# A GRU and block attention kernel: input tiles loaded first, the bias broadcast by DMA and added in PSUM

## The reference

```
gi = x_t @ W_ih + b_ih;   gh = h @ W_hh + b_hh           # 512 -> 1536 each
r = sigmoid(i_r + h_r);   z = sigmoid(i_z + h_z)
n = tanh(i_n + r * h_n);  h = (1 - z) * n + z * h        # 64 steps, one after another
x = x + hs
block = sum of x over 8 steps;  keys = rms_norm(block @ Wk.T) * rms_weight
attended = softmax(keys . cond[1]) over the blocks, applied to block
x = x + layernorm(x + attended @ Wo.T) * gamma + beta
```

## Time and profile before

| | us |
|---|---|
| median of three runs | 376.84 |
| the profiled execution | 376.77 |
| its span on the core, first to last instruction | 374.7 |
| TensorE busy in the span | 362.5 |
| VectorE, ScalarE, GpSimd busy | 262.6, 161.8, 16.1 |

### The profile page before, as it was taken

The page is one execution under the profiler, slowest core; times in us unless marked ns, Lnnn a source line. Parts: engine busy times, 40 slices in busy tenths (PEclk is TensorE's granted clock), DMA queues, the critical chain, the costliest instruction groups (busy, mean ns, idle before and its releaser), DMA issues.

```text
span 374.7 us, 9838 instructions
## 1 busy us (share of the span) xinstructions
PE 362.5 (97%) x3285; PEld 213.6 (57%) x3285; DVE 262.6 (70%) x1137; ACT 161.8 (43%) x512; POOL 16.1 (4%) x50
## 2 busy tenths in 40 slices
PE   7999999999999999999999999999999999997894
PEld 4465556666555566665556666555566665434662
DVE  3725667767676877686768767676878676778896
ACT  3702226262434344362526262434344364866510
POOL 7002000000000000000000000000000000100000
PEclk9999999999999999999999999999999999999999
DMA  5975535323232322324142323232232323110047
GB/s 186 396 298 119 159 96 163 101 70 100 73 97 71 74 73 67 101 52 113 34 108 49 98 70 98 70 98 70 58 89 67 101 52 78 42 42 20 21 169 280
DMA packets 27484, 38.63 MB, mean 103 GB/s; under 512 B 2988, under 2 KB 19016, under 8 KB 27464
## 3 DMA queue, kind: packets, MB, share of 16 engines
q1 hardware_dynamic: 27432, 38.36, 35.3%
q10 hardware_dynamic: 32, 0.01, 0.0%
HBM read 18.17 MB, written 4.19 MB: 60 GB/s over the span
## 4 chain that ended last, share of the span: by engine, by line
PE 92%; DVE 5%; issue 1%; DMA 1%; ACT 0%; DVEq 0%; SPq 0%
PE gates_ps L619 43%; PE gi_ps L587 37%; DVE gcx L1117 1%; PE first_ps L680 1%; PE first_ps L619 1%; PE fourth_ps L619 1%; PE third_ps L619 1%; PE keys_ps L619 1%; PE third_ps L680 1%; PE keys_ps L680 1%; PE fourth_ps L680 1%; DMA h_tok<-hist 1%; DVE w_hh L1032 1%; PE gi_ps L601 1%; PE keys_ps L747 1%
## 5 line engine op out<-in xcount | busy, mean ns | idle before, releaser
L619 PE MATMUL gates_ps<-w_hh,turned 128*32 128x384 f32 x1920 | 167.3, 489 | 0.5 <-DVE turned L840 0.5
L619 PEld LDWEIGHTS gates_ps<-w_hh,turned 128*32 128x32 f32 x1920 | 56.5, 109 | 85.5 <-issue 56.4
L587 PE MATMUL gi_ps<-w_ih_hi,xt_hi 128*128 128x384 f32 x240 | 87.3, 364 | 0.0
L587 PE MATMUL gi_ps<-w_ih_hi,xt_lo 128*128 128x384 f32 x240 | 81.2, 338 | 0.0
L587 PE MATMUL gi_ps<-w_ih_lo,xt_hi 128*128 128x384 f32 x240 | 80.2, 334 | 0.0
L480 ACT ACTIVATE rz<-gates_ps 128x256 f32<-128x256 f32 x60 | 23.0, 384 | 128.8 <-PE gates_ps L619 128.7
L904 DVE TENSOR_TENSOR rz<-gates_ps,rz 128x128 f32<-128x128 f32 x60 | 17.5, 292 | 79.5 <-ACT rz L480 79.5
L587 PEld LDWEIGHTS gi_ps<-w_ih_hi,xt_hi 128*128 128x128 f32 x240 | 45.0, 187 | 37.5 <-issue 37.5
L587 PEld LDWEIGHTS gi_ps<-w_ih_lo,xt_hi 128*128 128x128 f32 x240 | 45.1, 188 | 0.0
L587 PEld LDWEIGHTS gi_ps<-w_ih_hi,xt_lo 128*128 128x128 f32 x240 | 45.0, 187 | 0.0
L840 DVE STREAM_TRANSPOSE turned<-hist 128x32 f32<-128x32 f32 (+1 forms) x192 | 36.8, 217 | 2.2
(11 more groups left out here) (224 smaller groups left out, 301.1 us busy)
## 6 DMA issues: line engine op xcount, KB each, us to landing
gi<-gi_tok SPq DMA_DIRECT2D x60, 192.0 KB, 3.4
x1t<-in_x_t_dram SPq DMA_DIRECT2D x16, 256.0 KB, 3.2
gcx<-in_x_tok_dram SPq DMA_DIRECT2D x16, 256.0 KB, 3.2
h_tok<-hist SPq DMA_DIRECT2D x64, 64.0 KB, 2.2
out_dram<-gcx SPq DMA_DIRECT2D x16, 256.0 KB, 2.1
gcx<-in_w_ih_dram SPq DMA_DIRECT2D x4, 768.0 KB, 7.4
w_hh<-in_w_hh_dram SPq DMA_DIRECT2D x4, 768.0 KB, 9.1
wo_t<-in_wo_t_dram SPq DMA_DIRECT2D x1, 1024.0 KB, 5.6
```

Of the source, the lines that this page charges most:

```text
L587: mm = pe.matmul(gi_ps[tok][:, 0:G3], a[:, k, :], w[:, k, gi_cols(j)], start=(k == 0 and a is xt_hi and w is w_ih_hi), stop=(k == NJ - 1 a ...
L619: mm = pe.matmul(gates_bank(t)[j * B:(j + 1) * B, P:], before[:, k * B:(k + 1) * B], chunk(w_hh, k, j), start=False, stop=(k == NJ - 1), s ...
```

## The change

1. SP no longer waits first. Its order is: x's first quad, `W_ih` quarters 0 and 1, four broadcast transfers of the bias (32 partitions of 768 floats, 96 KB each), `W_ih` quarter 2, x's second quad, `W_ih` quarter 3, `cond`. `W_hh` and `b_in` follow as before; behind `b_hh_rz` stand six more transfers of constants (four of 64 KB, one of 512 KB, one of 256 KB).
2. The selection matrices, the small loads, the constants on TensorE and the copies of them are gone, the `lay_pick` between steps 0 and 1 too. TensorE has seven matmuls on zeros (L650) in place of three.
3. The first projection accumulates onto zeros. When quarter 1 has been added to bank t, VectorE adds the bias to it in place; TensorE waits for that before it adds quarter 2.
4. VectorE's order: low part of quarter 0, the sum of two bias parts, the four additions, low part of quarter 1, x's low part, low parts of 2 and 3, the turns of the first state. ScalarE rounds x before quarter 3. `gi_chunk(4)` takes the products with W's low part last, each behind a wait for its quarter.
5. `wq` and `wq_rec` are multiplied on GpSimd after its `b_in` sums; the waits on them, and the turn of beta, come later (step 3 in the first block). `br_all` and `br_t` lose a block that nothing wrote.

The core of the diff:

```diff
 # SP
-            sp.wait_ge(bias_made, 1)
-            sp.dma_start(bias_rows[0:NJ, 0:G3], b_ih_d).then_inc(bias_in, 16)
...
             sp.dma_start(x1t[:, 0], x_t_d[:, 0:NJ, :]).then_inc(x_first_in, 16)
             load_w_ih(0)
+            load_w_ih(1)
+            for j in range(NJ):
+                sp.dma_start(bias_in_rec[j * B:(j + 1) * B, :], bias_d[j:j + 1, :].broadcast_to([B, 6 * P])
+                             ).then_inc(bias_in, 16)
+            load_w_ih(2)
+            load_x_t(1)
+            load_w_ih(3)
             sp.dma_start(hist[:, S - 1, :], cond_d).then_inc(h0_in, 16)
-            load_w_ih(1)
-            load_w_ih(2)
-            load_w_ih(3)
-            load_x_t(1)
...
+            for j in range(NJ):
+                sp.dma_start(recs[j * B:(j + 1) * B].rearrange("p c u -> p (c u)"),
+                             recs_d[j:j + 1, :].broadcast_to([B, 4 * P])).then_inc(consts_in, 16)
+            sp.dma_start(tok_consts[:].rearrange("p c n -> p (c n)"), rows_d[None, 0:2 * D].broadcast_to([P, 2 * D])
+                         ).then_inc(consts_in, 16)
+            sp.dma_start(rms_tok, rows_d[None, 2 * D:].broadcast_to([P, D])).then_inc(consts_in, 16)
             move_gi(0, -1)
 # GpSimd
-            pool.memset(own_rows, 0.0).then_inc(pick_made, 1)
...
+            pool.tensor_tensor(wq, wq, rms_tok, ALU.mult).then_inc(wq_ready, 1)
+            pool.tensor_tensor(wq_rec, wq_rec, rms_rec, ALU.mult).then_inc(wq_ready, 1)
 # TensorE
-                if first and s == 0:
-                    lay_pick(small_ps, 2)
...
-            keep_warm(2)
...
-            keep_warm(1).then_inc(pe_warmed, 1)
+            keep_warm(7).then_inc(pe_warmed, 1)
...
+                    if k == 2:
+                        pe.wait_ge(first_seeded, t + 1)
                     for j in range(NJ):
...
+                    if k == 1:
+                        mm.then_inc(first_laid, 1)
...
-            gi_chunk(Q, Q, 1)
+            pe.wait_ge(w_hi_ready, NJ)
+            gi_chunk(Q, Q, 1, lo_last=True)
 # VectorE
+            split_w(0)
+            dve.wait_ge(bias_in, 16 * NJ)
+            dve.tensor_tensor(bias_rec[:, P:3 * P], bias_rec[:, P:3 * P], bias_in_rec[:, D:], ALU.add
+                              ).then_inc(bias_summed, 1)
+            dve.wait_ge(bias_summed, 1)
+            for t in range(Q):
+
+                dve.wait_ge(first_laid, t + 1)
+                dve.tensor_tensor(first_ps[t][:], first_ps[t][:], bias_rec, ALU.add).then_inc(first_seeded, 1)
+            split_w(1)
+            split_x(1)
+            split_w(2)
+            split_w(3)
             dve.wait_ge(h0_in, 16)
             for c in parts:
                 dve.transpose(turned[:, S - 1, c], hist[:, S - 1, c]).then_inc(ht_ready, 1)
-            for k in range(NJ):
-                split_w(k)
-            split_x(1)
```

More of the change, by code:

```diff
@@ L66, in gru_block_attention @@
         scalar_warm = sb("scalar_warm", [P, 1])
[L68 to L71, removed]
+        tok_consts = sb("tok_consts", [P, 2, D])
+        gamma_tok, wq = tok_consts[:, 0, :], tok_consts[:, 1, :]
+        recs = sb("recs", [P, 4, P])
+        gamma_rec, beta_rec, wq_rec, rms_rec = (recs[:, c, :] for c in range(4))
         beta_t = sb("beta_t", [P, P])
@@ L239, in steps @@
             def steps(i, first=False, last=False):
+                if last:
+                    sp.wait_ge(wq_ready, 2)
                 for s in range(S):
@@ L584, in gi_chunk @@
                 wait(pe, gi_tok_ready, idx - 1 - Q)
-                for k in range(NJ):
[L586 to L589, removed]
+                terms = ((xt_hi, w_ih_hi), (xt_hi, w_ih_lo), (xt_lo, w_ih_hi))
+                order = [(k, a, w) for k in range(NJ) for a, w in terms]
+                if lo_last:
+                    order = [(k, a, w) for a, w in (terms[0], terms[2], terms[1]) for k in range(NJ)]
+                for m, (k, a, w) in enumerate(order):
+                    if lo_last and w is w_ih_lo:
+                        pe.wait_ge(w_lo_ready, k + 1)
+                    mm = pe.matmul(gi_ps[tok][:, 0:G3], a[:, k, :], w[:, k, gi_cols(j)], start=(m == 0),
+                                   stop=(m == 3 * NJ - 1))
                 mm.then_inc(gi_done, 1)
@@ L651, in keep_warm @@
                 return mm
-            def lay_pick(bank, c):
-                for j in range(NJ):
-                    mm = pe.matmul(bank[:, j * P:(j + 1) * P], pick[:, j, :], const_rows[:, c, :],
-                                   start=True, stop=True)
-                mm.then_inc(consts_laid, 1)
-            keep_warm(2)
-            pe.wait_ge(pick_made, 4)
-            pe.wait_ge(bias_in, 48)
-            pe.matmul(first_ps[0][:], own_rows, bias_rows, start=True, stop=True).then_inc(bias_laid, 1)
-            pe.wait_ge(pick_made, 5)
-            pe.wait_ge(wq_row_ready, 1)
-            pe.matmul(gi_ps[0][:, 0:3 * P], own_rows, const_rows[:, 0:3, :], start=True, stop=True
-                      ).then_inc(consts_laid, 1)
-            lay_pick(gi_ps[1], 0)
-            keep_warm(1).then_inc(pe_warmed, 1)
+            keep_warm(7).then_inc(pe_warmed, 1)
             pe.wait_ge(x_first_in, 16)
@@ L1166 @@
     b_hh = by_chunk(inputs["L0_cond_b_hh"], (0, 1, 2))[0]
+    b_ih = by_chunk(inputs["L0_cond_b_ih"], (2, 0, 1)).reshape(NJ, G3)
+    rms, gamma, beta = (inputs[f"L1_cond_{name}"] for name in ("rms_weight", "ln_gamma", "ln_beta"))
     laid_out = {
@@ L1172 @@
         "w_ih": by_chunk(inputs["L0_cond_W_ih"], (2, 0, 1)).reshape(D, 3 * D), "w_hh": inputs["L0_cond_W_hh"],
-        "b_ih": by_chunk(inputs["L0_cond_b_ih"], (2, 0, 1)).reshape(NJ, G3),
-        "b_hh": _np.concatenate([b_hh[:, 0:2].reshape(-1), b_hh[:, 2].reshape(-1)]),
-        "rms_weight": inputs["L1_cond_rms_weight"],
+        "b_ih": b_ih,
+        "b_hh_rz": b_hh[:, 0:2].reshape(-1),
+        "bias": _np.concatenate([b_ih, b_hh[:, 2], b_hh[:, 0], b_hh[:, 1]], axis=1),
+        "recs": _np.concatenate([a.reshape(NJ, P) for a in (gamma, beta, cond[1], rms)], axis=1),
+        "rows": _np.concatenate([gamma, cond[1], rms]),
         "wk_t": inputs["L1_cond_Wk"].transpose(1, 0), "wo_t": inputs["L1_cond_Wo"].transpose(1, 0),
-        "gamma": inputs["L1_cond_ln_gamma"], "beta": inputs["L1_cond_ln_beta"],
     }
```

102 lines of the change are left out of this document (28 added, 74 removed).

## The result

| | before | after |
|---|---|---|
| median of the runs on one chip, 22 each | 377.37 us (376.36 to 378.64) | 375.72 us (375.10 to 377.35) |
| profiled execution | 376.77 us | 375.67 us |
| its span | 374.7 us | 373.5 us |
| TensorE's share of the chain | 92% | 85% |
| step 0 ends on TensorE | 25.07 us | 23.56 us |

The ratio on record is 0.9965, interval [0.9956, 0.9975]: 0.35% faster. The interval leaves out a ratio of 1, but the gain lies under the 0.5% that the prediction set as its bound for a change that one measurement of this kernel can tell. (The two medians stand 1.65 us apart, 0.44%.) I had put the likeliest time at 374.7 and "faster by over 0.5%" at 0.60; the median of the changed kernel lies one microsecond above that.

What follows compares the result with a forecast made beforehand. The prediction had TensorE and the DMA stream finish step 0 together, the `W_hh` transfers setting its end after the change. 1.25 (step 0) + 0.89 (`lay_pick`) = 2.14 us off 376.77 gave 374.63, stated as 374.7; range 372.8 to 376.1.

Steps and rivals of the forecast that it cites:

- the bound of step 0: Opening: the last quarter of `W_hh` lands at 22.95 us, so step 0 ends at 23.8 against 25.07, 1.25 earlier.
- TensorE's own path: Opening: TensorE's work alone, if nothing makes it wait, would end step 0 at 22.3 us.
- The `lay_pick`: Between steps 0 and 1: 0.89 us of TensorE with nothing beside it goes in full.
- The term of the bias: DMA stream ahead of `W_hh`: four bias transfers cost 1.3 us, with 0.98 and 2.8 as the ends.
- SP's start: Opening: SP issues x first, at 0.71 instead of 3.26 us, so x and quarter 0 land 2.55 earlier.
- the TensorE rival: Opening: a shorter DMA tail leaves TensorE as the bound, step 0 ending at 22.3 to 22.5, 373.2 us; chance 0.25.
- GpSimd's two products: Behind the opening: the two products fall in idle time of GpSimd and cost nothing.
- The prediction's list of signs: Wrong if, among others, `rz` L904 of step 1 is held by GpSimd or TensorE waits longer on VectorE than on `W_hh`.
- The slack of `b_in`: Before VectorE's `rz` of step 1: slack falls from 1.4 to 0.5 us, so `b_in` stays covered.
- The constants: Queue behind `b_in`: six transfers, 2.6 us, ahead of the first `move_gi`, which has until step 4.
- the bias was dear: Rival, DMA stream: bias transfers at 140 GB/s cost 2.8 us, leaving a gain of 0.64, 376.2 us; chance 0.21.
- `b_in` was not late: Rival, step 1: constants delay `b_in` by 3.8 us, making the kernel 1.2 us slower, 378.0; chance 0.04.

Runs made afterwards that it cites:

- the first experiment: The changed kernel with GpSimd's two products held until VectorE has made six projected rows: 375.47 us, ratio 0.9954; run again, 374.36 us.
- one-transfer kernel: The changed kernel with the same 0.39 MB of bias as one transfer to 128 partitions, rows repeated in DRAM: 375.83 us, ratio 0.9967.
- the first combined version: Changed kernel with one bias transfer, `b_in` and its summand in two halves, fourth sum behind the third kept rows, products later: 374.11 us, ratio 0.9916.
- the last version: The first combined version with constants issued in step 4, beta turned in step 6 and GpSimd's products in step 8: 374.13 us, ratio 0.9913.

## Why the prediction was half right

**What held.** SP's first issue came at 0.74 (forecast 0.7). `W_hh` was the bound of step 0, which ended at 23.56 (forecast 23.8), and TensorE's own path stood where it was put: 22.47 in the run without the bias, for 22.3. The `lay_pick` went in full: 0.89. Step 1 began at 25.84 (forecast 26.1), 2.42 us earlier where the sum said 2.14. Behind step 1 all steps but one kept the lengths that they had.

**The term of the bias was too small, and another gain made up for it.** I took 1.3 us between 0.98 and 2.8; the runs give 1.86. With SP's start alone, 2.55 earlier, that would have left 0.7 at the `b_in` issue; measured were 1.54, because the stream without the bias came 3.40 earlier, not 2.55 (22.37 against 18.97). I had that extra only among the reasons of the TensorE rival (no small loads between the first quarters, `cond` behind). The trace of before has room for it: the prediction read the stream as 329 to 423 GB/s "all the way", but it moved 248 in 4 to 6 us and 376 in 6 to 8, where the kernel without the bias, 2.5 us ahead of it, moved 369 in 2 to 4 us and 415 in 4 to 6. Which of the rearranged loads made that difference was not tested. Two errors of 0.56 and 0.85 stood against each other, so that step 0 ended near its forecast is in part luck; with the scatter of single executions (0.3 to 0.6 us at step 0) neither is exact.

The Trainium skill (SBUF — State Buffer, "Door 1: The DMA port swizzle") gave half the rate for 32 partitions, an estimate of 2.0 us in the prediction. The measured 1.86 agrees, and so does the 0.78 of the 128-partition form, less than half of it, with the reserve above that this form differs in more than its partitions. I had leaned away from the rule because four queued transfers "can overlap"; the price leaves no room for that.

**The step that failed** is the sentence that GpSimd's two products "fall in idle time of their engines: nothing". They did fall in idle time of GpSimd. But the product of 29.67 to 30.96 held the VectorE instruction beside it that reads two operands in SBUF, the `zh` of step 1, until its own end, and this `zh` stands ahead of the state on the path that TensorE waits for. Step 2 began at 31.96 instead of 30.9: 1.1 us of the 2.42 were lost, and 1.0 of them is the products' price where the prediction has nothing. Moving them gives 1.0 back, putting them on step 3 takes 1.05 there, a clear in their place takes nothing. The prediction's list of signs had GpSimd only as what `rz` waits for, by a late sum, and not as what holds an instruction that waits for nothing.

The Trainium skill (SBUF — State Buffer, "Who interferes with whom") states just this: a VectorE instruction with two SBUF inputs contends with a GpSimd instruction that reads SBUF, and not with one that only writes. The runs agree with it in each part: 1.25 and 1.23 us beside the product in steps 1 and 3, 0.25 beside the clear, and `gi_tok` with its one SBUF operand never above 0.56. The prediction used the rule on ports for the transfers and left out this one on the two engines.

**The slack of `b_in`** was forecast at 0.5 and was 0.25, since step 1 came 0.3 us sooner than forecast and GpSimd's sums only 0.05 (they began 1.30 us earlier than in before, for 1.25). It covered the landing. It did not cover the reading: the last sum lies across the first `zh`, which takes 0.18 us alone, 0.39 here, 0.56 in the first experiment and 0.73 with the one transfer. That is where the remaining 0.14 us of step 1 in the first experiment and 0.27 with one transfer and the product later go.

**The constants** "ahead of the first `move_gi`", which "has until step 4": that held as long as the move went out late. With a short step 1 and `b_in` loaded whole, the move was issued at 27.36 to 28.52 us, and VectorE waited at most 0.46 us for it, and step 2 kept its 5.02. In the first combined version the split `b_in` let it go out at 26.43, and VectorE waited 2.34 us on it in step 2, since it keeps its next rows in the place that the move empties. And the `gi` rows came 2.6 us late in step 4 when the constants went behind the second move. I counted who needs the rows and not who needs their place.

**The sum, with what was measured:** 1.51 (step 0) + 0.89 = 2.4 to step 1; less 1.1 in step 1 and 0.1 between steps 15 and 16: 1.2 us, and 1.2/376.8 is 0.32%, where the ratio says 0.35%. With the first term as forecast and the product known, the sum would have been 2.14 - 1.1 = 1.04, or 375.7, and "no change that can be told" the likeliest case. Of the rivals, none happened as told: TensorE did not become the bound, the bias was dear but not at 2.8, and `b_in` was not late.

**Left open.** The step from 15 to 16, the first that a loop's jump back leads into, took 5.02 us in before, 5.03 in the first experiment, 5.13 in after, 5.12 in the kernel before without its `lay_pick`, 5.17 in the last version, and 5.36 and 5.37 in the one-transfer and the first combined kernel. It varies with no edit near it, and no GpSimd instruction lies near it either (the closest in after ends at 80.1 us, this step begins at 100). In after its chain shows 0.06 us of issue ahead of the step's matmuls and no releaser, and in the one-transfer kernel VectorE's usual instructions with pauses of issue between them. And the clock fall in the last part was seen, not provoked.

## What to carry to other kernels

Work put on an idle engine is free only if it holds no engine beside it. Here two GpSimd products that nobody waited for took 1.0 us from VectorE: give GpSimd's SBUF reads a stretch in which VectorE has no instruction with two SBUF operands on the path. When the edge between two steps is tight (0.25 us here), list what each new instruction overlaps, not only who waits for it. For every transfer placed ahead of another in a queue, ask who needs that other one's data and also who needs the buffer that it empties.

## What the hardware showed that I had not expected

- A 128x96 VectorE product of two SBUF operands took 1.25 us beside a GpSimd product of 128x512, and 0.25 beside a GpSimd clear of the same size or alone. VectorE was held until the other ended: 29.83 to 31.08 beside 29.67 to 30.96, and in the four other profiles in which the product starts just ahead of a `zh` of this size, the `zh` ends 0.11 us after it as well.
- 0.39 MB cost a full queue 0.78 us as one transfer into 128 partitions and 1.86 as four into 32 each (0.8 to 1.15 and 1.7 to 2.2 over all profiles).
- The rise of TensorE's clock to the 2.4 GHz level does not come at one place. TensorE's work up to the projection is the same in after and in the kernel without the bias transfers, and both start it at 1.55 us. In after the seven matmuls of 512 columns took 2.30 us and the projection ran at full speed from 5.82 on; without the bias they took 3.19 (2.99 up to the start of the next, so 0.43 each, the 1.2 GHz level), and the first group of the projection was slow too:

```profile
3.42 2.30 PE L630 MATMUL gates_ps<-xt_hi 128*128 128x512 f32 x7
5.82 0.88 PE L642 MATMUL first_ps<-gcx,x1t 128*32 128x384 f32 x8
...
3.43 3.19 PE L627 MATMUL gates_ps<-xt_hi 128*128 128x512 f32 x7
6.55 1.25 PE L639 MATMUL first_ps<-gcx,x1t 128*32 128x384 f32 x8
```

  Over the eleven profiles with seven such matmuls they took 2.30 to 3.19 us. The prediction's place for the rise, 7.4 us, fits the slow ones. What moved it was not tested; in after it stayed hidden behind the transfers.
- In some executions the granted clock falls to 0.50, the 1.2 GHz level, for about 2 us in the last part, after a stretch in which TensorE was busy 0.41 of 2.00 us. The same kernel without the fall has the same idle stretch (0.40 of 2.00). It costs 1.4 us each time.
